# Moving the multiply of the upper half (decay times sine) from VectorE to GpSimd in the first stage of a vision-tower kernel

## The reference, cut to what matters

```python
dtA = A * dt[:, None]
Cc = Cc * (jnp.exp(dtA) - 1.0) / A
V = jnp.exp(dtA[:, :, None] * ell)                      # ell = 0 .. 1023
K = 2.0 * jnp.einsum('chn,hnl->chl', Cc, V).real
h = K
h = h + attention(layernorm(h))
h = h + feed_forward(layernorm(h))
```

## Time and profile before

| | before |
|---|---|
| median of 3 runs (lowest to highest) | 2920.29 us (2919.62 to 2920.88) |
| span of the profiled execution | 2918.6 us |
| median less that span | 1.7 us |
| first stage: from the start to the last copy of its rows | about 208 us |
| distance between two chunks, at the lower multiply L493 | 10.8 to 11.9 us |

### The profile page before, as it was taken

One profiled execution on the slowest core, in us unless ns is written; L12 is line 12 of the kernel. 1 busy time (PEld: TensorE's weight loads), 2 busy tenths in 40 slices (PEclk: granted clock), 3 DMA queues, 4 the chain that ended last, 5 costly groups with the idle time before them and its releaser, 6 DMA issues.

```text
span 2918.6 us, 61988 instructions
## 1 busy us (share of the span) xinstructions
PE 2813.4 (96%) x16932; PEld 1397.8 (48%) x16932; DVE 2487.8 (85%) x8774; ACT 1918.7 (66%) x5987; POOL 1968.9 (67%) x1731
## 2 busy tenths in 40 slices
PE   6788899999999999999999999999999999999987
PEld 5665444444444444444444444444444444444433
DVE  9987788888888888888888888888888888888874
ACT  8987766666666666666666666666666666666652
POOL 3533676777677777777777776677767777677763
PEclk9999899999999999999999999999999999999999
DMA  7885676666666666666666666666666666666762
GB/s 245 234 215 139 134 155 149 148 148 148 153 144 150 148 148 150 149 148 149 150 148 143 150 148 154 149 143 151 145 155 148 148 148 146 152 147 150 143 131 63
DMA packets 1220852, 442.64 MB, mean 152 GB/s; under 512 B 1167121, under 2 KB 1175569, under 8 KB 1220641
## 3 DMA queue, kind: packets, MB, share of 16 engines
q1 hardware_dynamic: 1220640, 440.69, 67.1%
HBM read 88.22 MB, written 67.11 MB: 53 GB/s over the span
## 4 chain that ended last, share of the span: by engine, by line
PE 89%; DVE 3%; ACT 3%; DMA 2%; issue 1%; POOL 1%; SPq 0%; ACTq 0%; DVEq 0%; POOLq 0%
PE bank_b L1781 45%; PE bank_a L1781 22%; PE bank_c L1781 11%; PE score L1746 4%; PE pv L1770 3%; PE kps L581 1%; DMA tok_h<-kout 1%; PE pv L1885 1%; ACT kout L358 1%; ACT probs L1351 1%; ACT v L333 1%; PE pv L1841 0%; PE bank_c L1841 0%; DVE z L506 0%; DVE z L507 0%
## 5 line engine op out<-in xcount | busy, mean ns | idle before, releaser
L1351 ACT ACTIVATE probs<-probs,negmax 128x128 f32<-128x128 f32 x2048 | 790.0, 387 | 233.2 <-DVE negmax L1503 233.1
L1264 POOL TENSOR_TENSOR p_hl<-probs,p_hl 128x512 f16<-128x512 f32 x512 | 613.9, 1199 | 342.1 <-ACT p_hl L1360 338.3
L1260 POOL TENSOR_TENSOR probs<-probs,rsum 128x512 f32<-128x512 f32 x512 | 556.4, 1087 | 226.0 <-DVE rsum L1514 226.0
L1781 PE MATMUL bank_a<-qkv_hi,xt 128*128 128x512 f16 x2048 | 652.8, 380 | 1.9 <-DMA xt<-xy_hl 1.9
L1503 DVE CUSTOM_DVE_ANT_0 probs<-score,table,scal 128x128 f32<-128x128 f32 x2048 | 601.1, 348 | 35.6 <-issue 31.4
L1781 PE MATMUL bank_b<-b_hi,yt 128*128 128x512 f16 x2016 | 631.5, 380 | 0.0
L1360 ACT ACTIVATE p_hl<-probs 128x512 f16<-128x512 f32 x512 | 319.9, 625 | 414.3 <-POOL probs L1260 414.3
L1557 DVE TENSOR_TENSOR heads<-rope_a,heads 128x512 f16<-128x512 f32 x320 | 412.8, 1306 | 29.9 <-ACT heads L1381 29.8
L1781 PE MATMUL bank_b<-o_hi,at_hi 128*128 128x512 f16 x1024 | 389.2, 380 | 1.5 <-ACT at_hi L1366 1.5
L1781 PE MATMUL bank_a<-qkv_lo,xt 128*128 128x512 f16 x1024 | 389.3, 380 | 0.0
L1781 PE MATMUL bank_b<-o_lo,at_hi 128*128 128x512 f16 x1024 | 389.1, 380 | 0.0
(11 more groups left out here) (220 smaller groups left out, 4530.1 us busy)
## 6 DMA issues: line engine op xcount, KB each, us to landing
hin<-tok_h SPq DMA_DIRECT2D x64, 512.0 KB, 3.3
r<-tok_h SPq DMA_DIRECT2D x64, 512.0 KB, 3.9
out_dram<-r SPq DMA_DIRECT2D x63, 512.0 KB, 2.9
tok_h<-kout SPq DMA_DIRECT2D x60, 512.0 KB, 6.1
probs_t<-p_hl SPq DMA_TRANSPOSE x512, 3.1
xc<-in_x_dram SPq DMA_DIRECT2D x32, 128.0 KB, 4.3
raw_a<-in_L_attn_wq_dram SPq DMA_DIRECT2D x4, 1024.0 KB, 8.9
raw_b<-in_L_attn_wo_dram SPq DMA_DIRECT2D x8, 512.0 KB, 4.6
```

The source lines that it names most:

```text
L1260: TT(x, x, rsum[:, u % 4].unsqueeze(2).to_broadcast([P, GR, T]), ALU.mult).then_inc(s_norm, 1)
L1264: TT(p_hl[:, u % 2, 1], probs[:, u % 4], p_hl[:, u % 2, 0], ALU.subtract).then_inc(s_plo, 1)
L1351: ins = A(probs[:, u % 4, g], probs[:, u % 4, g], ACT.Exp, bias=negmax[:, u % 4, g:g + 1], scale=-1.0, accum_out=sums[:, u % 4, g:g + 1])
L1781: ins = MM(bank, x(c), w[:, c, cols], start=(c == 0 and i == 0), stop=(c == KC - 1 and i == 2))
```

## The change

The upper multiply leaves VectorE. GpSimd does it at the start of its body, ahead of the addition of the same chunk, after waits for the decay and the sine; a new semaphore `s_vu` tells that the upper half is ready. The lower half stays on VectorE (`s_v`). Whoever waited for `s_v` waits for `s_vu` as well: VectorE before it writes the next angle into `u`, TensorE before the rows of a chunk, and two waits in the weight preparation behind the last chunk. In the last chunk GpSimd multiplies too, where it had nothing to do before.

```diff
-    s_v = sem("v_ready")
+    s_v = sem("v_lower_ready")
+    s_vu = sem("v_upper_ready")
...
-            elif not (isinstance(ch, int) and ch == NCH - 1):
+            else:
+                pool.wait_ge(s_e, ch + 1)
+                pool.wait_ge(s_sin, ch + 1)
+                upper = v[:, r, :, LH:L0]
+                nc.gpsimd.tensor_tensor(upper, upper, u[:, r], ALU.mult).then_inc(s_vu, 1)
+            if exists(ch) and not (isinstance(ch, int) and ch == NCH - 1):
                 pool.wait_ge(s_z12, ch + 1)
                 pool.wait_ge(s_v, ch + 1)
...
                 if exists(ch - 1):
                     dve.wait_ge(s_v, ch)
+                    dve.wait_ge(s_vu, ch)
...
-                upper, lower = v[:, r, :, LH:L0], v[:, r, :, 0:LH]
-                TT(upper, upper, u[:, r], ALU.mult)
+                lower = v[:, r, :, 0:LH]
                 STT(lower, u[:, r, :, ::-1], const[:, C_SIGN:C_SIGN + 1], lower, ALU.mult, ALU.mult).then_inc(s_v, 1)
...
         def rows(ch, r, h0, h1):
             pe.wait_ge(s_v, ch + 1)
+            pe.wait_ge(s_vu, ch + 1)
...
                 if j == 0:
                     act.wait_ge(w["s_v"], NCH)
+                    act.wait_ge(w["s_vu"], NCH)
...
+                    if j == 0:
+                        dve.wait_ge(w["s_vu"], NCH)
```

More of the change, by code:

```diff
@@ L155, in token_kernel @@
     s_kev = sem("k_copied")
-    w.update(raw_b=raw_b, z_first=z[:, 0].rearrange("p h m b -> p (h m b)"), wide=wide, ar_raw=ar_raw, s_z12=s_z12, s_z=s_z, s_v=s_v, s_kev=s_kev)
+    w.update(raw_b=raw_b, z_first=z[:, 0].rearrange("p h m b -> p (h m b)"), wide=wide, ar_raw=ar_raw, s_z12=s_z12, s_z=s_z, s_v=s_v, s_vu=s_vu, s_kev=s_kev)
     s_kp = sem("k_in_psum")
```

## The result

The changed kernel takes 2934.82 us (median of five runs; four lie between 2932.46 and 2937.65, and their own median is 2934.48) against 2920.29: 1.0047 times the time before, 95% interval 1.0034 to 1.0059. A fifth run of 7928.01 us, with a mean granted clock of 0.53, is not in that ratio. 2934.5 was forecast. The profiled execution has a span of 2936.0 us, 17.4 more than the 2918.6 of the one before; its run took 2937.65 us, the longest of those four.

The account below looks back on a forecast made before the run. It took VectorE, in turns with GpSimd at SBUF, as the stage's bound. 3.9 + 6.1 + 4.6 + 0.9 - 1.3 = 14.2 us on a span of 2918.6, plus 1.7 to the median, gave 2934.5 us, range 2924.5 to 2941.

Parts of the forecast that it names:

- The turns of VectorE and GpSimd: From L477 to L493 of each chunk, VectorE and GpSimd take turns at SBUF, so GpSimd has no spare time there.
- The lower multiply: L493, never seen beside GpSimd, was let be held as L477 was; if not held, the sum falls by 6 us.
- the sum by the row: Holds taken from L477 at 34.15, held 1.96 of 2.09 us left; the skill's rule would add about 3 us.
- The steady part: Chunk 2 to 14: six even bodies 6.1, five odd 4.6, body 13 0.9, less 1.3 us of VectorE's matmul waits.
- odd body: GpSimd body with L516: the multiply holds L480 some 2.04 us, less 1.13 saved, net +0.91 us.
- even body: GpSimd body without L516: the multiply holds L493, which starts at 131.70 instead of 130.68, +1.02 us.
- The start: Chunk 0's multiply queues behind GpSimd's load-delayed copies, its addition is late, and L493 of chunk 2 comes 3.9 us later.
- VectorE's wait before `u`: VectorE's wait ahead of writing the next angle is for the chunk before, long done, so costs nothing.
- Behind the stage: After the stage nothing changes; the part behind it is shifted whole.
- Rival 1: GpSimd's time is really free and the stage gets shorter: 2918.5 us, or 2905.6 if no other loop held; chance 0.09.
- Rival 2: Part of the multiply finds free time, as when L493 is not held or ScalarE's sine is late: 3.9 to 8 us slower; chance 0.16.
- Rival 3: VectorE runs L477 to L493 through, the multiply comes after: 1.2 us a chunk or more lost, some 2940; chance 0.13.

Follow-up runs that it names:

- e2: Kernel before, VectorE's upper multiply kept, plus a further GpSimd multiply of two constants whose result nobody reads: 2947.25 us, ratio 1.0087.
- e3: Changed kernel with the GpSimd multiply replaced by a memset of the same size and GpSimd's loop written out: 2924.34 us, ratio 1.0010 to the kernel before.
- e7: Changed kernel, but GpSimd multiplies only the even chunks from chunk 2 on, VectorE the rest: 2932.41 us, ratio 1.0037 to the kernel before.
- e6: Changed kernel, but GpSimd multiplies only the odd chunks, VectorE the even ones: 2925.27 us, ratio 1.0016 to the kernel before.
- e4: Changed kernel without any upper multiply on either engine and without the waits for `s_vu`: 2925.50 us, ratio 1.0016 to the kernel before.
- e11: e4 with TensorE repeating the turns of the coefficients twice more: 2925.50 us, ratio 1.0013 to the kernel before.
- e13_even_warm: e7 with TensorE repeating the turns of the coefficients twice more: 2935.28 us, ratio 1.0050 to the kernel before.

## Why the prediction was right, point by point

*The turns of VectorE and GpSimd* were read from the earlier trace rows and are shown: the instructions named were held, 1.98 and 2.10 us against 2.04 and 2.15 forecast; e2 shows the hold without any change of the dataflow, and e3 that a two-operand instruction is not held when GpSimd does not read. The lower multiply, which was in doubt, is held like the rest. The Trainium skill's rule that the second to come stands still for the whole instruction ("SBUF — State Buffer", "SBUF: two separate sides") would have had it at 2.36 us; the holds are 0.26 and 0.38 us less, and the sum by the row was the nearer one.

*The steady part* was put at 10.3 us from chunk 2 to 14; it is 144.47 - 134.54 = 9.9. That the two bodies can be summed, 1.02 and 0.91, was right in result but not as a rule: alone, the multiply in the odd body (e7) costs 1.72, through ScalarE, and the even body's adds only 0.11 to it. The weak step is the one where the sum treats VectorE's loop as the only one. In the changed kernel the ring over the late sine and VectorE's own loop end within 0.2 us of each other, so the sum over either gives the pair; that they do is luck, and nothing in the prediction foresaw it.

*The start* was put at 3.9 and is 3.76 counted from the end of the copies. The path was partly another: I wrote that VectorE's wait before `u` was long done, and at the start it is not. L484 of body 1 waited 2.92 us for the multiply of chunk 0, and then the addition went first and L484 took 3.29. That the sum came out alike is luck.

*Behind the stage* nothing was to change. The profiled execution has 1.6 us more there, so 5.83 + 9.93 + 1.64 = 17.4; between the profiled executions of the table that part varies by more than this.

*Rival 1* (GpSimd's time is free) is out by e2 and e6. Its price was also too good: a multiply that costs nothing gives 2925.5, not 2918.5. *Rival 2*: L493 was held, and a sine that came late (the multiply waited 0.51 us for it in the body shown) cost nothing. *Rival 3*: they took turns. Open stay two things: why e4 with less work is 0.16% slower than the kernel before, and the stop behind the stage in e11. The lower clock is a part of the first: in e4's chain sixteen rows take up to 5.42 us instead of 3.73, and its pairs take 22.84 us in the mean against 22.25 with the clock kept up. It is not the whole, since e11 too is slower than before.

## What to carry to other kernels

Before an element-wise step goes from VectorE to GpSimd, look at what VectorE does at that moment: here the two took turns beside VectorE instructions with two SBUF operands and beside the whole-turns `tensor_scalar`, and 2.36 us on GpSimd replaced 1.13 on VectorE; only beside the instructions that read PSUM (2.28 us either way) and beside the reduction (1.21) was GpSimd's work hidden. Lengthened VectorE instructions next to GpSimd work are the sign, and a busy share counts them as work. And before pricing a gain, run the kernel with the step left out: here that showed that there was nothing to win, because a second ring of the same length, which passes ScalarE's copies, TensorE's rows and VectorE's angle but not the multiply, took up all that VectorE was spared. Last, two costs in one loop may be added only if they lie on the same ring: e6 and e7 give 0.95 and 1.72 us apart and 1.83 together.

## What the runs showed of the hardware that was not expected

A GpSimd memset of 128x1024 floats took 0.95 us and left the two-operand instruction beside it at 1.22 us, but held the one-operand `tensor_scalar` (0.75 us for 1024 columns) some 0.23 us. The holds by the multiply, 2.10 and 1.98 us, are 0.26 and 0.38 us shorter than it is as recorded (2.36). After a pause of TensorE of 3.33 us the granted clock of the next 4 us was 0.58 (e7_even); with the pause cut to 1.58 by transposes it was 1.00 (e13_even_warm). With VectorE relieved, keeping the clock up was worth 0.6 us per pair in the mean (22.84 to 22.25), 0.80 in the middle pair and nothing in the one before it (21.97 both); in the changed kernel it was worth nothing (24.08 and 24.10).
